# Moving VectorE's LayerNorm statistics of x1 from the front of a scan tile to its middle, with the power on GpSimd that follows them

## The chip, the cores and the metric

The kernel runs on one NeuronCore of a Trainium2 chip. The metric is the device time of one execution in microseconds (us). Below, PE is the matmul engine (TensorE), DVE is VectorE, ACT is ScalarE, POOL is GpSimd, and SP only issues DMAs. A trace of one execution shows when each instruction of each engine ran.

## What is computed

The block is a Mamba-2 mixer with an MLP, a LayerNorm, a gated ternary feed-forward network and a second LayerNorm, over 2 sequences of 2048 tokens with 256 features, in float32. Cut to what matters here:

```python
h   = x + mamba2(rmsnorm(x), ...)          # scan over chunks, 8 heads of 64
m   = square(relu(rmsnorm(h) @ w_fc)) @ w_proj
x1  = layernorm(x + (h + m))               # (v - mean) / sqrt(var + 1e-5)
f   = silu(x1 @ w1) * (x1 @ w2)
f   = gelu(gelu(f @ h1) @ h2) @ w3
out = layernorm(x1 + f)
```

## The kernel before

The 4096 tokens are 8 tiles of 512 tokens. A tile is 4 chunks of 128 tokens, one per pass of the partitions. Stage one, the scan, goes over the tiles in order (about the first half of the time) and writes x1 to DRAM. Stage two reads it back and does the feed-forward network; the change does not touch it.

In the scan each engine runs its own `iteration`, a list of calls written out by hand. Nothing reorders it: an engine does its instructions in the order in which they stand, and waits on semaphores for the others. The iteration of tile i mixes three tiles. It does the scan of tile i, the projection and convolution of tile i+1, and the MLP of tile i-1. The LayerNorm of x1 runs one tile further behind, for tile i-2. Tile 0 and tile 1 have no such LayerNorm, tiles 2 to 6 are one hardware loop, and tile 7 is written out by itself.

A chunk c of the scan passes through these steps (lines of the kernel before). PE makes the decay exponents (`exponents`, L665, called dlo and dhi), DVE clamps them into `E` (`mask_exponents`, L1448), ACT takes the exponential, and DVE multiplies with the scores (`scores`, L1458). PE's `y_diag` (L690) waits for that product and for `u`, which POOL makes (`make_u`, L1264). PE's `y_off` (L682) reads the state `S`. DVE adds the two (`y_off` L1466, `y_diag` L1477 and L1479) and gates the sum (`gate`, L1500). PE transposes it (`turn_y`, L703), ACT and DVE split it into a high and a low part (`yT`, DVE's L1351), PE multiplies by `w_out` (`out_rows`), and DVE adds the residual (`add_out`, L1511). After chunk 3, PE transposes `h` (`turn_h`, L720), DVE writes its low part (`hT`, also L1351), and PE's first MLP matmul (`fc(w, 0)`, L579 with `hT`) waits for it. POOL decays the state (`decay_state`, L1287) and makes `ud` (`make_ud`, L1271). DVE also runs 18 convolution taps per tile (`tap`, L1372) and normalizes the next x (`norm_x`, L1358). `ud` and the decay of chunk 3 are used by PE's `state(w, i, 3)` and DVE's `state`.

PSUM banks rotate. DVE's items share three banks, so PE may start an item only when DVE has drained the item three places before: dhi3 waits until `yT0` has been drained by L1351.

The part that is moved: `norm_x1` computes the LayerNorm statistics of x1, four BN_STATS (L177) and seven instructions on 128x4 values (L183 to L189), and signals `s_mv`. POOL's `x1_rstd` (L237) waits for `s_mv` and raises the variance to the power -0.5. DVE's `scale_x1` (L242), late in the tile, waits for POOL's result and writes x1, which SP stores.

Of the kernel before, what the change touches and what calls it, by code (L numbers as in the profile page):

```python
# [29 lines left out]
CH = TILE // P  # L30
# [15 lines left out]
EPS_LN = 1e-05  # L46
# [85 lines left out]
def post_ln_block(nc, x, x_t, w_in, conv_w, conv_b, dt_bias, a_log, d_skip, norm_w, w_out, w_fc, w_proj,  # L132
# [16 lines left out]
    with ctx:  # L149
        def sb(name, shape, dt=F32, into=ctx):  # L150
            return into.enter_context(nc.sbuf_tensor(name, shape, dt))

        def sem(name):
            return ctx.enter_context(nc.semaphore(name))
# [18 lines left out]
        def layer_norm_stats(step, src, bn, mv, eps):  # L173


            for c in range(CH):
                step.mark(nc.vector.bn_stats(bn[:, c, :], src[:, c, :]))  # L177
            step.wait(step.n)
            return layer_norm_tail(step, bn, mv, eps)

        def layer_norm_tail(step, bn, mv, eps):
            tt, ts = nc.vector.tensor_tensor, nc.vector.tensor_scalar
            step.mark(tt(mv[:, 0, :], bn[:, :, 1], bn[:, :, 4], ALU.add))  # L183
            step.mark(tt(mv[:, 2, :], bn[:, :, 1], bn[:, :, 4], ALU.subtract))
            step.link(tt(mv[:, 1, :], bn[:, :, 2], bn[:, :, 5], ALU.add))
            step.mark(ts(mv[:, 0, :], mv[:, 0, :], 0.5, None, ALU.mult))
            step.mark(tt(mv[:, 2, :], mv[:, 2, :], mv[:, 2, :], ALU.mult))
            step.link(ts(mv[:, 1, :], mv[:, 1, :], 1.0 / D, eps, ALU.mult, ALU.add))
            return nc.vector.scalar_tensor_tensor(out=mv[:, 1, :], in0=mv[:, 2, :], scalar=0.25,  # L189
                                                  in1=mv[:, 1, :], op0=ALU.mult, op1=ALU.add)  # L190

        STAT_STEPS = CH + 6
# [25 lines left out]
        def sum_x1(dve, t):  # L218

            dve.wait_ge(s_pj, KH * t + KH)  # L220
            dve.wait_ge(s_r2h, t + 1)
            dve.wait_ge(s_x1o, 16 * t + 1)
            dve.wait_ge(s_xh, t + 1)
            for c in range(CH):
                nc.vector.scalar_tensor_tensor(
                    out=x1[:, c, :], in0=pj_banks[c // 2][:, (c % 2) * D:(c % 2 + 1) * D],
                    scalar=r2h[:, c:c + 1], in1=xh[:, c, :], op0=ALU.mult, op1=ALU.add).then_inc(s_pjd, 1)

        def norm_x1(dve, t):
            step = Steps(dve, s_ls, STAT_STEPS * t)  # L230
            dve.wait_ge(s_pjd, CH * t + CH + 1)
            layer_norm_stats(step, x1, bn, mv, EPS_LN).then_inc(s_mv, 1)
            assert step.n == STAT_STEPS

        def x1_rstd(pool, t):
            pool.wait_ge(s_mv, t + 1)
            nc.gpsimd.tensor_tensor(rsv[:], mv[:, 1, :], eps[:, 3:4].broadcast_to([P, CH]), ALU.pow).then_inc(s_rsv, 1)  # L237
# [39 lines left out]
        bn, mv, rsv = sb("bn", [P, CH, 6]), sb("mv", [P, 3, CH]), sb("rsv", [P, CH])  # L277
        x1 = sb("x1", [P, CH, D])
# [32 lines left out]
        s_pjd = sem("proj_drained")  # L311
        s_xh = sem("x_plus_h_ready")
        s_r2h = sem("h_rstd_ready")
        s_mv = sem("ln_var_ready")
        s_rsv = sem("ln_rstd_ready")
        s_ls = sem("ln_step")
# [133 lines left out]
        with nc.Block() as block:  # L450
# [758 lines left out]
            def _(pool):  # L1209
# [36 lines left out]
                def m_lo_part(t, j):  # L1246
                    pool.wait_ge(s_mh, KH * t + j + 1)
                    nc.gpsimd.tensor_tensor(m_lo[:, j % MB, :], m_fc[:, j % 2, :], m_hi[:, j % MB, :].bitcast(F32),  # L1248
                                            ALU.subtract).then_inc(s_ml, 1)

                def chunk_totals(i):
                    pool.wait_ge(s_dec, i + 1)
                    nc.gpsimd.tensor_tensor(dec[:, 2, :], dec[:, 0, :], dec[:, 1, :], ALU.mult).then_inc(s_tot, 1)
# [7 lines left out]
                def make_u(w, i, c):  # L1261
                    turned_x(w, i, c)
                    ge(pool, s_si, CH * i + c - 1)
                    nc.gpsimd.tensor_tensor(heads(u[:, c % 2, :]), heads(xt[:, c % 2, :]),  # L1264
                                            bc(dt[:, c * HEADS:(c + 1) * HEADS]), ALU.mult).then_inc(s_u, 1)

                def make_ud(w, i, c):
                    pool.wait_ge(s_u, CH * i + c + 1)
                    if c == 0:
                        pool.wait_ge(s_dec, i + 1)  # L1270
                    nc.gpsimd.tensor_tensor(heads(ud[:, c % 2, :]), heads(u[:, c % 2, :]),  # L1271
                                            bc(dec[:, 1, c * HEADS:(c + 1) * HEADS]), ALU.mult).then_inc(s_ud, 1)

                def make_skip(w, i, c):
                    turned_x(w, i, c)
                    if c >= 2:
                        pool.wait_ge(s_rsy, CH * i + c - 1)
                        pool.wait_ge(s_di, w.dve(f"yT{c - 2}") + 1)
                    nc.gpsimd.tensor_tensor(heads(y[:, c % 2, :]), heads(xt[:, c % 2, :]), bc(dskip_b[:]),
                                            ALU.mult).then_inc(s_skip, 1)  # L1280

                def decay_state(i, c):
                    b, o = c % 2, 1 - c % 2
                    pool.wait_ge(s_sup, CH * i + c + 1)
                    if c == 0:
                        pool.wait_ge(s_tot, i + 1)
                    nc.gpsimd.tensor_tensor(heads(S[:, o, :]), heads(S[:, b, :]),  # L1287
                                            bc(dec[:, 2, c * HEADS:(c + 1) * HEADS]), ALU.mult).then_inc(s_sdec, 1)

                def iteration(w, i, mlp, more, norm):  # L1290
                    make_skip(w, i, 0)
                    make_u(w, i, 0)
                    chunk_totals(i)
                    if mlp:
                        m_lo_part(i - 1, 2)
                    make_ud(w, i, 0)
                    if mlp:
                        decay_state(i, 0)
                    else:
                        pool.wait_ge(s_tot, 1)  # L1300
                    make_u(w, i, 1)
                    make_skip(w, i, 1)
                    make_ud(w, i, 1)
                    decay_state(i, 1)
                    if norm:
                        x1_rstd(pool, i - 2)
                    make_u(w, i, 2)
                    make_u(w, i, 3)
                    make_ud(w, i, 2)
                    decay_state(i, 2)  # L1310
                    make_skip(w, i, 2)
                    if mlp:
                        m_lo_part(i - 1, 4)
                    make_skip(w, i, 3)
                    if mlp:
                        m_lo_part(i - 1, 6)
                    if more:
                        make_ud(w, i, 3)
                        decay_state(i, 3)
                    m_lo_part(i, 0)  # L1320
                    if more:
                        decay_operands(w, i + 1)
# [9 lines left out]
            def _(dve):  # L1332
# [15 lines left out]
                def lo_part(w, name, hi, lo):  # L1348

                    dve.wait_ge(s_hi, w.hi(name) + 1)  # L1350
                    nc.vector.tensor_tensor(lo, banks[w.dve_bank(name)][:], hi.bitcast(F32),  # L1351
                                            ALU.subtract).then_inc(s_dd, 1)
# [149 lines left out]
                def yT(w, c):  # L1502
                    lo_part(w, f"yT{c}", flat3(yT_hi), flat3(yT_lo))

                def add_out(w, i, c):
                    b = item(w, f"wo{c}")
                    dve.wait_ge(s_rsy, CH * i + c + 1)
                    if c == 0:
                        dve.wait_ge(s_xres, 16 * i + 16)
                        ge(dve, s_r2h, i)  # L1510
                    nc.vector.scalar_tensor_tensor(out=h[:, c, :], in0=b[:, 0:D], scalar=rsy[:, c:c + 1],  # L1511
                                                   in1=x_res[:, c, :], op0=ALU.mult, op1=ALU.add).then_inc(s_dd, 1)
# [15 lines left out]
                def iteration(w, i, before, more, norm):  # L1528
                    mlp = before is not None
                    per = F_STEPS + CM_STEPS  # L1530
                    step = Steps(dve, s_ds, HEAD_STEPS + per * i - (1 if mlp else 0))
                    if norm:
                        norm_x1(dve, i - 2)
                    mask_exponents(w, 0)
                    if mlp and not norm:
                        turn_squares(i)
# [50 lines left out]
                    if more:  # L1587
                        tap(step, w, i + 1, 4, 1)
                    add_out(w, i, 1)
                    yT(w, 2)  # L1590
                    y_diag(step, w, i, 3)
                    if more:
# [37 lines left out]
                    if mlp:  # L1630
                        sum_x1(dve, i - 1)
# [18 lines left out]
                step = Steps(dve, s_ds, 0)  # L1650
# [437 lines left out]
```

## Time and profile before

| | us |
|---|---|
| median of 3 runs (1225.24 to 1225.66) | 1225.28 |
| the profiled execution | 1226.21 |
| its span, first to last instruction | 1224.50 |
| PE busy in the span | 1195.6 (98%) |
| DVE busy | 783.8 (64%) |
| ACT busy | 639.2 (52%) |
| POOL busy | 237.7 (19%) |

The profiled execution has 1.71 us around its span. DVE's 64% is an average over two unlike stages: in the scan its busy tenths are 8 and 9, in the second stage 3 to 6. Ends of matmuls are modelled, so PE may show as busy while it waits a little; where a matmul starts is what to read.

### The profile page before, as it was taken

To read this page: it belongs to the slowest core of one execution; us is meant where nothing else is said; L and a number is where in the kernel's file an instruction comes from. 1 tells how busy PE (TensorE), PEld (TensorE's weight loads), DVE (VectorE), ACT (ScalarE), POOL (GpSimd) and SP (SyncE) were. 2 spreads that over 40 slices of the span, in tenths; PEclk is the share of its full clock that TensorE was granted. 3 is DMA by queue.
4 is the path that set the end of the run, shared out by engine and by line. 5 is a ranking of instruction groups with operands and counts; after the bars stand their busy time and mean duration, and the time that the engine had idled before them with its cause. 6 is when DMAs were issued, how large, how long until landed. Compare 5 with 4: busy or idle time off the path is not lost.

```text
span 1224.5 us, 19168 instructions
## 1 busy us (share of the span) xinstructions
PE 1195.6 (98%) x6412; PEld 1003.1 (82%) x6412; DVE 783.8 (64%) x1370; ACT 639.2 (52%) x1199; POOL 237.7 (19%) x210
## 2 busy tenths in 40 slices
PE   8899999999999999999999999999999999999996
PEld 7677888888887888788888888888888888888885
DVE  6798898989999898855535337345363363543633
ACT  6687888878788878666224124142141331422420
POOL 0517253443435261720000000000000000000000
PEclk9999999999999999999999999999999999999998
DMA  8214131333324141334500202002002020020000
GB/s 294 71 65 126 65 81 72 105 99 101 105 78 128 58 124 64 99 128 172 211 1 1 52 1 51 0 0 51 0 6 45 0 51 0 0 51 0 18 1 19
DMA packets 92169, 79.40 MB, mean 65 GB/s; under 512 B 63200, under 2 KB 81760, under 8 KB 90208
## 3 DMA queue, kind: packets, MB, share of 16 engines
q1 hardware_dynamic: 92128, 78.86, 20.8%
q8 instruction: 25, 0.41, 0.1%
q14 instruction: 16, 0.13, 0.0%
HBM read 66.77 MB, written 25.70 MB: 76 GB/s over the span
## 4 chain that ended last, share of the span: by engine, by line
issue 53%; POOL 0%; DVE 0%; POOLq 0%; DVEq 0%
POOL rsv_b L1937 0%; DVE o_sb L2014 0%; POOLq L1935 0%; DVEq L1768 0%; POOL rsv L237 0%; POOLq L450 0%
## 5 line engine op out<-in xcount | busy, mean ns | idle before, releaser
L1921 ACT ACTIVATE full<-bank,scale 128x512 f32<-128x512 f32 x128 | 88.3, 690 | 383.0 <-PE bank L1830 383.0
L1830 PE MATMUL bank<-hB_hi,h_sb 128*128 128x512 f32 x512 | 199.6, 390 | 0.0
L1830 PE MATMUL bank<-hB_lo,h_sb 128*128 128x512 f32 x512 | 199.6, 390 | 0.0
L1830 PE MATMUL bank<-hA_hi,h_sb 128*128 128x512 f32 x512 | 199.3, 389 | 0.0
L1830 PE MATMUL bank<-hA_lo,h_sb 128*128 128x512 f32 x512 | 199.3, 389 | 0.0
L1983 DVE CAST hA_hi<-full 128x512 fp32r<-128x512 f32 x64 | 27.3, 427 | 173.1 <-ACT full L1921 173.1
L1937 POOL TENSOR_TENSOR rsv_b<-mv_b,eps 128x4 f32<-128x4 f32 x8 | 10.7, 1340 | 618.2 <-DVE mv_b L189 618.2
L1830 PEld LDWEIGHTS bank<-hA_hi,h_sb 128*128 128x128 f32 x512 | 96.1, 188 | 20.1
L1830 PEld LDWEIGHTS bank<-hA_lo,h_sb 128*128 128x128 f32 x512 | 96.1, 188 | 20.1
L1830 PEld LDWEIGHTS bank<-hB_hi,h_sb 128*128 128x128 f32 x512 | 96.3, 188 | 19.2
L1830 PEld LDWEIGHTS bank<-hB_lo,h_sb 128*128 128x128 f32 x512 | 96.2, 188 | 19.0
L1372 DVE SCALAR_TENSOR_TENSOR xc<-xp,conv_w_sb,xc 128x512 f32<-128x512 f32 x144 | 104.4, 763 | 0.5
L1950 DVE TENSOR_TENSOR hA_lo<-full,hA_hi 128x512 fp32r<-128x512 f32 x128 | 88.0, 687 | 3.0
L1983 DVE CAST hB_hi<-full 128x512 fp32r<-128x512 f32 x64 | 27.1, 424 | 97.7 <-ACT full L1921 97.7
L1957 DVE SCALAR_TENSOR_TENSOR full<-bank,scale,gate 128x512 f32<-128x512 f32 x64 | 48.0, 751 | 63.1 <-PE bank L1830 62.9
L579 PE MATMUL bank<-w_pj_hi,m 128*128 128x256 f32 x256 | 81.7, 319 | 0.0
L1914 ACT ACTIVATE gate<-bank,scale 128x512 f32<-128x512 f32 x64 | 44.1, 689 | 60.5 <-PE bank L1830 60.5
L1248 POOL TENSOR_TENSOR m<-m_fc,m 128x512 fp32r<-128x512 f32 x29 | 43.7, 1506 | 162.2 <-ACT m L1044 162.2
L581 PE MATMUL bank<-w_pj_hi,m 128*128 128x256 f32 x256 | 72.4, 283 | 0.0
L580 PE MATMUL bank<-w_pj_lo,m 128*128 128x256 f32 x256 | 72.3, 282 | 0.0
L690 PEld LDWEIGHTS bank<-u,E 128*128 128x128 f32 x512 | 60.2, 192 | 10.8 <-issue 10.5
L1830 PE MATMUL bank<-w_sb,hA_hi 128*128 128x256 f32 x256 | 63.1, 283 | 0.0
(231 smaller groups left out, 2967.6 us busy)
## 6 DMA issues: line engine op xcount, KB each, us to landing
chk_xh<-w_ffn SPq DMA_DIRECT2D x16, 704.0 KB, 4.2
ffn_raw<-w_ffn SPq DMA_DIRECT2D x8, 1408.0 KB, 7.0
h_sb<-ffn_raw SPq DMA_DIRECT2D x2, 4096.0 KB, 19.0
xT<-x_t SPq DMA_DIRECT2D x8, 512.0 KB, 3.9
x_res<-x SPq DMA_DIRECT2D x8, 512.0 KB, 3.8
x_rows<-x SPq DMA_DIRECT2D x8, 512.0 KB, 3.5
x_in<-x_rows SPq DMA_DIRECT2D x8, 512.0 KB, 4.7
x_in<-x SPq DMA_DIRECT2D x7, 512.0 KB, 4.7
```

The source lines that it names most:

```text
L579: pe.matmul(o, lo, rhi, start=first, stop=False, skip_group_check=True)
L580: pe.matmul(o, hi, rlo, start=False, stop=False, skip_group_check=True)
L581: return pe.matmul(o, hi, rhi, start=False, stop=last, skip_group_check=True)
L690: last = pe.matmul(b[:, hs], E[:, c % 2, n, :], u[:, c % 2, hs], start=True, stop=True)
L1248: nc.gpsimd.tensor_tensor(m_lo[:, j % MB, :], m_fc[:, j % 2, :], m_hi[:, j % MB, :].bitcast(F32), ALU.subtract).then_inc(s_ml, 1)
L1372: ins = nc.vector.scalar_tensor_tensor(out=xc[:, m, :], in0=xp[:, m, n:n + TILE], scalar=conv_w_sb[:, m, n:n + 1], in1=xc[:, m, :], op0=AL ...
L1830: ins = pe.matmul(o, a_, b_, start=first and n == 0, stop=last and n == 1, skip_group_check=True)
L1914: nc.scalar.activation(gate[:, j % 2, :], b[:], ACT.Silu, scale=scale[:, 0, j:j + 1]).then_inc(s_gd, 1)
L1921: nc.scalar.activation(full[:, n % FULL, :], b[:], ACT.Gelu, scale=scale[:, 1 + n // KH, n % KH:n % KH + 1]).then_inc(s_gd, 1)
L1950: nc.vector.tensor_tensor(lo, full[:, n % FULL, :], hi.bitcast(F32), ALU.subtract).then_inc(s_split, 1)
L1957: nc.vector.scalar_tensor_tensor(out=full[:, j % FULL, :], in0=t_bank(KD + j)[:], scalar=scale[:, 1, j:j + 1], in1=gate[:, j % 2, :], op0= ...
L1983: nc.vector.tensor_copy(hi[:, n % KH, :], full[:, n % FULL, :]).then_inc(s_shi, 1)
```

## The change

DVE: `norm_x1` no longer stands at the front of the iteration (before the first mask of the exponents). The same eleven instructions, split into two functions, now stand after `add_out(w, i, 1)` and before `yT(w, 2)`. POOL: `x1_rstd` no longer stands between `decay_state(i, 1)` and `make_u(w, i, 2)`. It stands after `m_lo_part(i - 1, 6)`, before `make_ud(w, i, 3)` and `decay_state(i, 3)`. `scale_x1` and the store stay. The copy of `norm_x1` that runs after the last tile stays.

```diff
+        def stats_x1(dve, t):
+            step = Steps(dve, s_ls, STAT_STEPS * t)
+            dve.wait_ge(s_pjd, CH * t + CH + 1)
+            for c in range(CH):
+                step.mark(nc.vector.bn_stats(bn[:, c, :], x1[:, c, :]))
+            return step
+
+        def norm_x1_tail(step):
+            step.wait(step.n)
+            layer_norm_tail(step, bn, mv, EPS_LN).then_inc(s_mv, 1)
+            assert step.n == STAT_STEPS
...
                     decay_state(i, 1)
-                    if norm:
-                        x1_rstd(pool, i - 2)
                     make_u(w, i, 2)
...
                         m_lo_part(i - 1, 6)
+                    if norm:
+                        x1_rstd(pool, i - 2)
                     if more:
                         make_ud(w, i, 3)
                         decay_state(i, 3)
...
-                    if norm:
-                        norm_x1(dve, i - 2)
                     mask_exponents(w, 0)
...
                     add_out(w, i, 1)
+                    if norm:
+                        x1_step = stats_x1(dve, i - 2)
+                    if norm:
+                        norm_x1_tail(x1_step)
                     yT(w, 2)
```

The 13 new lines shift the numbers of all later lines by 13 (L1264 becomes L1277).

POOL in the loop over tiles 2 to 6, from the decay of chunk 1 on, before (`u` is `make_u` of chunks 2 and 3, `rsv` is the power):

```order
L1287 TENSOR_TENSOR S<-S,dec 128x512 [waits state_updated]
L237 TENSOR_TENSOR rsv<-mv,eps 128x4 [waits ln_var_ready]
L1257 REGISTER_ALU
L1264 TENSOR_TENSOR u<-xt,sm 128x512 [waits state_item_ready,turned_x_of_chunk_2_loaded]
L1264 TENSOR_TENSOR u<-xt,sm 128x512 [waits state_item_ready,turned_x_of_chunk_3_loaded]
```

The same place of POOL now:

```order
L1300 TENSOR_TENSOR S<-S,dec 128x512 [waits state_updated]
L1270 REGISTER_ALU
L1277 TENSOR_TENSOR u<-xt,sm 128x512 [waits state_item_ready,turned_x_of_chunk_2_loaded]
L1277 TENSOR_TENSOR u<-xt,sm 128x512 [waits state_item_ready,turned_x_of_chunk_3_loaded]
L1281 REGISTER_ALU
```

`u` of chunk 2 now follows the decay of the state directly; the power no longer stands between them.

POOL later in the same tile, now, from the MLP's low part of block 6 on (before, the power's row was not there):

```order
L1261 TENSOR_TENSOR m<-m_fc,m 128x512 [waits m_hi_ready]
L250 TENSOR_TENSOR rsv<-mv,eps 128x4 [waits ln_var_ready]
L1281 REGISTER_ALU
L1284 TENSOR_TENSOR ud<-u,dec 128x512 [waits u_ready]
L1300 TENSOR_TENSOR S<-S,dec 128x512 [waits state_updated]
```

`ud` and the decay of chunk 3 are now queued behind a wait for DVE's statistics.

DVE in the middle of the tile, now, from chunk 1's output on (before, the first row was followed at once by the row of `yT_lo`):

```order
L1524 SCALAR_TENSOR_TENSOR h<-bank,stat,x_res 128x256 [waits y_rstd_ready,dve_item_ready]
L232 ISA
L234 BN_STATS bn<-x 128x6 [waits proj_drained]
L234 BN_STATS bn<-x 128x6 x3
L168 ISA
L183 TENSOR_TENSOR mv<-bn 128x4 [waits ln_step]
```

After it come the other six small instructions of the statistics, and then chunk 2's `yT_lo`, `y_diag` and gate, in the order of before.

## Rows read from the trace of the kernel before

**Rows 1.** Busy time by stretch, tile 2 and tile 7: us, PE, PEld, DVE, ACT, POOL, clock.

```profile
161.43:228.05 66.62, 66.29 (x408) 55.93 (x407) 59.45 (x99) 54.31 (x112) 28.67 (x24) 1.00 0.33 96
...
494.70:545.00 50.30, 47.21 (x313) 39.97 (x312) 39.63 (x66) 31.81 (x67) 22.32 (x19) 1.00 0.31 96
```

**Rows 2.** PE's instructions in time, first half of tile 2: start, us, instruction [idle before].

```profile
170.21 1.97 PE L690 MATMUL bank<-u,E 128*128 128x64 f32 x16
...
179.78 1.97 PE L690 MATMUL bank<-u,E 128*128 128x64 f32 x16
...
182.32 0.50 PE L665 MATMUL bank<-to_l,from_s 128*128 128x512 f32 x1 [0.28 <-DVE yT_lo L1351]
```

**Rows 3.** DVE's instructions in time, first half of tile 2.

```profile
162.14 1.40 DVE L177 BATCH_NORM_STATS2 bn<-x 128x6 f32<-128x256 f32 x4
...
165.27 0.17 DVE L189 SCALAR_TENSOR_TENSOR mv<-mv 128x4 f32<-128x4 f32 x1
...
168.78 1.33 DVE L1458 TENSOR_TENSOR E<-E,GB 128x1024 f32<-128x1024 f32 x1
...
177.02 1.53 DVE L1500 TENSOR_TENSOR y<-tmp,z_s 128x512 f32<-128x512 f32 x1
178.47 1.21 DVE L1458 TENSOR_TENSOR E<-E,GB 128x1024 f32<-128x1024 f32 x1
...
180.20 1.46 DVE L1358 TENSOR_TENSOR xT<-xT,x_rstd 128x1024 f32<-128x1024 f32 x1
```

**Rows 4.** POOL's instructions in time, first half of tile 2.

```profile
167.98 1.04 POOL L1287 TENSOR_TENSOR S<-S,dec 128x512 f32<-128x512 f32 x1
...
176.57 1.42 POOL L1287 TENSOR_TENSOR S<-S,dec 128x512 f32<-128x512 f32 x1 [2.42 <-DVE S L1488]
177.96 1.48 POOL L237 TENSOR_TENSOR rsv<-mv,eps 128x4 f32<-128x4 f32 x1
```

**Rows 5.** All engines in time, the same place in tile 1, which has no power.

```profile
109.93 1.49 POOL L1264 TENSOR_TENSOR u<-xt,sm 128x512 f32<-128x512 f32 x1
...
110.44 2.06 DVE L1458 TENSOR_TENSOR E<-E,GB 128x1024 f32<-128x1024 f32 x1
...
113.91 1.23 DVE L1358 TENSOR_TENSOR xT<-xT,x_rstd 128x1024 f32<-128x1024 f32 x1 [0.81 <-DMA x_rstd<-x_rstd_row]
```

**Rows 6.** DVE's instructions in time, second half of tile 2.

```profile
202.12 0.48 DVE L1511 SCALAR_TENSOR_TENSOR h<-bank,stat,x_res 128x256 f32<-128x256 f32 x1 [0.79 <-PE bank L581]
204.58 0.69 DVE L1351 TENSOR_TENSOR yT_lo<-bank,yT_hi 128x512 fp32r<-128x512 f32 x1 [1.98 <-ACT yT_hi L907]
...
206.50 0.69 DVE L1479 TENSOR_TENSOR tmp<-tmp,y 128x512 f32<-128x512 f32 x1
...
208.38 2.07 DVE L1372 SCALAR_TENSOR_TENSOR xc<-xp,conv_w_sb,xc 128x512 f32<-128x512 f32 x3
...
211.02 0.69 DVE L1351 TENSOR_TENSOR yT_lo<-bank,yT_hi 128x512 fp32r<-128x512 f32 x1 [0.18 <-ACT yT_hi L907]
...
215.66 0.48 DVE L1511 SCALAR_TENSOR_TENSOR h<-bank,stat,x_res 128x256 f32<-128x256 f32 x1
...
218.03 1.28 DVE L1351 TENSOR_TENSOR hT<-bank,hT 128x512 fp32r<-128x512 f32 x2
```

**Rows 7.** The tile `mv`: durations in ns, min/median/max over the kernel.

```profile
L185 DVE TENSOR_TENSOR mv<-bn x8: 153/1011/1016, 163.9 to 589.4; 128x4 f32<-128x4 f32 x8
...
L237 POOL TENSOR_TENSOR rsv<-mv,eps x8: 1006/1452/1476, 178.0 to 590.2; 128x4 f32<-128x4 f32 x8
```

**Rows 8.** DVE's instructions in time, tile 0.

```profile
68.98 4.10 DVE L1372 SCALAR_TENSOR_TENSOR xc<-xp,conv_w_sb,xc 128x512 f32<-128x512 f32 x3
```

**Rows 9.** PE's instructions in time, end of tile 2.

```profile
209.75 0.60 PE L703 MATMUL bank<-ident,y 128*128 128x128 f32 x4
...
216.68 1.03 PE L720 MATMUL bank<-ident,h 128*128 128x128 f32 x8
...
219.62 0.39 PE L579 MATMUL bank<-hT,w_fc_lo 128*128 128x512 f32 x1
```

## The prediction

> **What bounds the kernel now.** I read the busy shares first: PE 98%, DVE 64%. Then the stretches by tile [rows 1]: in the scan DVE is busy 59.5 of 66.6 us per tile, so 64% understates it there. PE is busy 66.3 of 66.6 us. So PE sets the time, the waits it has left are small, and DVE follows with little slack. Moving DVE work can therefore save next to nothing, but it can cost as soon as one DVE result comes too late for PE. Third, I read PE, DVE and POOL side by side in time for tile 2; tiles 3 to 6 repeat it 66.6 to 66.7 us apart. Three places matter.
>
> At 182.32 PE waits 0.28 us for `yT_lo` of chunk 0 [rows 2]. This is the only wait that the first half of the tile shows as such. At 179.78 PE starts `y_diag` of chunk 1 [rows 2]; it needs the scores product that ends at 178.47 + 1.21 = 179.68 [rows 3], so that product has no more than 0.1 us in hand. At 219.62 PE starts the first MLP matmul [rows 9], which needs `hT_lo`, ended at 218.03 + 1.28 = 219.31 [rows 6]: 0.3 us in hand.
>
> **How POOL and DVE share.** The DVE products whose two inputs both lie in SBUF and POOL's products take turns. The gate runs from 177.02 for 1.53 us [rows 3], though the same form takes 0.69 (L1479 at 206.50 [rows 6]); it ends 0.56 us after POOL's `S` ends at 176.57 + 1.42 = 177.99 [rows 4]. POOL in turn wins the next turn if it is waiting when DVE's product ends: `S` was ready at 176.57 and got in before the gate. Instructions that read PSUM, such as `yT_lo`, keep their 0.68 us.
>
> **The front of the tile, removed.** Four BN_STATS and seven small instructions go from 162.14 to 165.27 + 0.17 = 165.44, 3.3 us of DVE [rows 3]. What was late behind them? The masks come earlier, so PE's `y_off` of chunk 0 can start some 0.14 us sooner. But `y_diag` of chunk 0 at 170.21 [rows 2] follows the scores product, which ends at 168.78 + 1.33 = 170.11 [rows 3]. That is 1.09 us after POOL's decay of `S` ends at 167.98 + 1.04 = 169.02 [rows 4], and the decay does not move: POOL's chain before it waits for ACT, not for the statistics. So the gain at `y_off` is taken back at `y_diag`. I take 0 per tile, with a bound of 0.3 if DVE gets ahead of POOL there (0.14 and another 0.15 that `y_diag` waits).
>
> **POOL's power, removed from 177.96.** Its 1.48 us hardly hold back DVE: the scores product beside it runs 1.21 us, its fastest form [rows 3, 4]. It works as a spacer. When it goes, `make_u` of chunk 2 is ready at 178.0, waits for the gate to end at 178.55, and takes the turn before the scores product of chunk 1. Tile 1 has no power and shows exactly this: `u` from 109.93 to 111.42, the scores product 2.06 us long, ending 1.08 after `u` [rows 5]. Price: 2.06 - 1.21 = 0.85 us. Behind the product on DVE stand `y_off` 1, `norm_x` and `yT_lo` 0. `norm_x` gets back 1.46 - 1.23 = 0.23, since `u` no longer runs beside it [rows 3, 5]. PE's `y_diag` 1 starts 0.85 late, at 180.63, and its exponents at 182.32 come with `yT_lo`, 0.85 - 0.23 = 0.62 later. From there all engines are shifted by 0.62 alike, since POOL's next `u` and DVE's next product wait for PE. Five loop tiles: 5 x 0.62 = 3.1 us. Bounds: 0 (the product wins the turn) and 0.85 each. I take 0.62, for tile 1 measured both halves.
>
> [...]
>
> **The middle, DVE.** `add_out` 1 ends at 202.60, and DVE then idles 1.98 us until 204.58 [rows 6]. The statistics cost 3.3 us at the front, of which L185 alone waits 1.011 - 0.153 = 0.86 for POOL [rows 7]; here POOL is done early, so 2.4 us. They end at about 204.95, `yT_lo` 2 runs 0.3 to 0.4 late, and DVE's wait for PE behind it (L1479 starts at 206.50 in both cases) absorbs that. By themselves the statistics are hidden.
>
> **The middle, POOL.** The power starts at 205.0 and takes 1.01 us when it waits for nothing [rows 7]. Queued behind it stand `ud` 3 and the decay of chunk 3. Before, both were done when L1479 started at its free 0.69 [rows 6]; now `ud` runs 206.05 to 207.1 (1.04, as `S` in rows 4). L1479 at 206.50 must wait for it: it ends at 207.1 + 0.56 = 207.65 instead of 207.19. The decay goes next, 207.65 to 208.55 (0.9 us, as `u` behind the gate in rows 5). The tap waits: 209.1. The gate of chunk 3 follows, 209.7. Before, it ended where the next taps begin, about 208.45 [rows 6]. So DVE is 1.25 us late. That taps do pay for this is seen in tile 0, where three of them beside `ud` and the decay take 4.10 us [rows 8] instead of 2.07 [rows 6].
>
> PE's `turn_y` 3 at 209.75 [rows 9] is just reached. DVE recovers some 0.27 before `yT_lo` 3, where it idled for ACT [rows 6], and stays 1.0 late from there, as nothing else in its queue waits. `add_out` 3 ends at 216.14 + 1.0 = 217.14 [rows 6]; PE's `turn_h` at 216.68 [rows 9] starts 0.5 late. `hT_lo` ends at 219.31 + 1.0 = 220.31, so the MLP matmul of 219.62 starts at 220.36, 0.74 late in all. Later DVE waits for PE again and its lateness is gone. Five tiles: 5 x 0.74 = 3.7 us. Bounds: 0 (POOL's two products find gaps) and 1.25 each. I take 0.74.
>
> **Tile 7.** It has no taps and no `ud` 3, and PE idles 3.1 of its 50.3 us [rows 1], so most of the 0.85 at its scores product is covered. I take 0.2 between 0 and 0.85.
>
> **Sum.** 3.1 + 3.7 + 0.2 = 7.0 us. The profiled execution takes 1226.21 us, 1.71 more than its span, and would take 1233.2. It lies 0.93 above the median of 1225.28, so the median becomes 1232.3 us.
>
> **Rivals.** *(a) Only the early turn is lost.* If `ud` and the decay fit between DVE's instructions, or DVE's slack at the end is larger than I read, the second half costs 0: 1225.3 + 3.3 = 1228.6. For it: I place the power to 0.1 us by adding durations. Against: two POOL products of 1 us must go through a stretch in which DVE is busy without a gap.
>
> *(b) Only the late turn is lost.* If the scores product gets its turn before `u` 2, the first half costs 0: 1225.3 + 3.7 = 1229.0. Against it: tile 1 [rows 5].
>
> *(c) Nothing is seen.* Both are covered, PE keeps its chain: 1225.3.
>
> *(d) Faster.* The place is the first half. If the scores products win both turns, PE gains 0.29 at `y_off` 0 and `y_diag` 0 and 0.23 at 182.32, since `norm_x` and so `yT_lo` come earlier: 0.52 x 5 = 2.6 us, 1222.7. It decides once the product is ready before POOL's decay at 167.98. For it: DVE is relieved by 3.3 us just there, and the 1.98 us gap takes the block. Against it: the product also needs `y_off` from PE, which PE starts no more than 0.14 us earlier.
>
> *(e) Worse.* Both lose at their bounds, because the waits of PE add up rather than overlap: 5 x (0.85 + 1.25) + 0.85 = 11.4 us, 1236.7.
>
> **Chances.** Forecast (both turns lost) 0.50, (a) 0.14, (b) 0.10, (c) 0.11, (d) 0.07, (e) 0.08. The range 1226.0 to 1237.0 holds all but (c), (d) and a little beyond (e). A measurement of this kernel tells about 0.2% from no change, 2.45 us. Slower by more: forecast, (a), (b), (e), 0.82. Within: (c), 0.11. Faster: 0.07.
>
> **What would show it.** In tiles 2 to 6 of the changed kernel: the scores product of chunk 1 takes about 2.06 us instead of 1.21, with `u` 2 right before it; PE's `y_diag` 1 starts that much later after `turn_y` 0; `y_diag` 0 stands as before relative to the tile's start. BN_STATS follow `add_out` 1, and the whole block takes about 2.4 us. The power takes about 1.0; DVE's L1479 waits for `ud` 3 and takes about 1.15; the gate of chunk 3 ends some 1.2 us later; PE waits for DVE before `turn_h` and before the first MLP matmul. The tile's period becomes 68.0 us (66.6 + 0.62 + 0.74). The forecast is wrong if that period stays at 66.6, if the scores product keeps 1.21, or if PE's granted clock leaves 1.00 [rows 1]. The second stage should take what it took.

## The result and the profile after

| us | before | after |
|---|---|---|
| median of 5 runs each | 1225.24 | 1232.68 (1229.93 to 1234.35) |
| ratio, 95% interval | | 1.006 [1.0046, 1.0074] |
| the profiled execution | 1226.21 | 1233.16 |
| its span | 1224.5 | 1231.4 |

The change costs 0.6%: 7.4 us by the medians, 6.9 us by the spans of the two profiled executions. The forecast was 1232.3, slower.

The same view as in [rows 1], now of the changed kernel: busy time by stretch, for tile 2 and tile 7. (The stretch of tile 7 in [rows 1] begins 0.10 us after that tile's first matmul, so its length isn't compared here.)

```profile
161.60:229.50 67.90, 66.82 (x407) 55.78 (x406) 60.17 (x99) 54.34 (x112) 29.90 (x24) 1.00 0.31 94
501.06:551.50 50.44, 47.41 (x312) 40.07 (x311) 39.95 (x66) 31.62 (x67) 23.01 (x19) 1.00 0.32 94
```

Tile 2 takes 67.90 instead of 66.62 us. PE's busy time rises by only 0.5, so the rest is waiting. The clock stays at 1.00. All five loop tiles do the same, 67.87 to 67.90 against 66.62 to 66.66 before: from the start of tile 2 to the start of tile 7 it is 339.46 instead of 333.17 us, 6.3 more. Tile 7 adds 0.23 at its first MLP matmul. That is 6.5 of the 6.9 us by which the span grew. Tile 2 itself starts 0.17 later, and the remaining 0.2 comes after that matmul of tile 7; the runs don't say why.

All engines in time, changed kernel, tile 2 (lines are 13 higher than before, and those of the matmul helpers too). In this view and the others of all engines below I print the rows of POOL and DVE, and the rows of PE that matter; what PE, its weight loads, ACT and SP do between them is left out, and "..." stands for left-out rows of POOL and DVE. First the place of POOL's removed power:

```profile
168.18 1.04 POOL L1300 TENSOR_TENSOR S<-S,dec 128x512 f32<-128x512 f32 x1
...
168.79 1.51 DVE L1471 TENSOR_TENSOR E<-E,GB 128x1024 f32<-128x1024 f32 x1
...
176.76 1.43 POOL L1300 TENSOR_TENSOR S<-S,dec 128x512 f32<-128x512 f32 x1 [2.42 <-DVE S L1501]
177.21 1.53 DVE L1513 TENSOR_TENSOR y<-tmp,z_s 128x512 f32<-128x512 f32 x1
...
178.16 1.49 POOL L1277 TENSOR_TENSOR u<-xt,sm 128x512 f32<-128x512 f32 x1
178.66 2.06 DVE L1471 TENSOR_TENSOR E<-E,GB 128x1024 f32<-128x1024 f32 x1
...
180.82 1.97 PE L703 MATMUL bank<-u,E 128*128 128x64 f32 x16 [0.70 <-issue]
181.25 1.21 DVE L1371 TENSOR_TENSOR xT<-xT,x_rstd 128x1024 f32<-128x1024 f32 x1
```

The gate at 177.21 is as long as before. Behind it, the scores product of chunk 1 takes 2.06 us, not the 1.21 of [rows 3]: POOL's `u`, which stood behind the power [rows 4], now starts at 178.16, ahead of it. These are tile 1's numbers [rows 5]. PE's `y_diag` 1 follows the product with 0.70 us of idle time. The view puts this on "issue", but it starts 0.10 us after the end of the product (178.66 + 2.06 = 180.72), which it needs; the spacer experiment below shows that the product was the cause. `norm_x` then runs 1.21 instead of 1.46. At the front, PE's `y_off` 0 starts 0.06 us earlier in the tile (5.34 instead of 5.40), but the scores product of chunk 0 takes 1.51 and ends at 170.30, still 1.08 behind POOL's decay (169.22), and `y_diag` 0 stands at 8.81 us in the tile (8.78 before).

Second, the middle and the end of the tile:

```profile
202.91 0.49 DVE L1524 SCALAR_TENSOR_TENSOR h<-bank,stat,x_res 128x256 f32<-128x256 f32 x1 [0.78 <-PE bank L594]
203.32 1.40 DVE L234 BATCH_NORM_STATS2 bn<-x 128x6 f32<-128x256 f32 x4
...
205.44 0.16 DVE L189 SCALAR_TENSOR_TENSOR mv<-mv 128x4 f32<-128x4 f32 x1
205.54 0.69 DVE L1364 TENSOR_TENSOR yT_lo<-bank,yT_hi 128x512 fp32r<-128x512 f32 x1
205.69 1.03 POOL L250 TENSOR_TENSOR rsv<-mv,eps 128x4 f32<-128x4 f32 x1 [0.83 <-DVE mv L189]
206.57 0.69 DVE L1490 TENSOR_TENSOR y<-y,bank 128x512 f32<-128x512 f32 x1 [0.33 <-PE bank L703]
206.69 1.04 POOL L1284 TENSOR_TENSOR ud<-u,dec 128x512 f32<-128x512 f32 x1
207.29 0.99 DVE L1492 TENSOR_TENSOR tmp<-tmp,y 128x512 f32<-128x512 f32 x1
207.69 1.49 POOL L1300 TENSOR_TENSOR S<-S,dec 128x512 f32<-128x512 f32 x1
208.20 1.53 DVE L1385 SCALAR_TENSOR_TENSOR xc<-xp,conv_w_sb,xc 128x512 f32<-128x512 f32 x1
209.66 0.68 DVE L1513 TENSOR_TENSOR y<-tmp,z_s 128x512 f32<-128x512 f32 x1
...
210.55 0.60 PE L716 MATMUL bank<-ident,y 128*128 128x128 f32 x4
...
217.80 1.09 PE L733 MATMUL bank<-ident,h 128*128 128x128 f32 x8
...
219.64 1.28 DVE L1364 TENSOR_TENSOR hT<-bank,hT 128x512 fp32r<-128x512 f32 x2
...
220.98 0.50 PE L592 MATMUL bank<-hT,w_fc_lo 128*128 128x512 f32 x1
```

The statistics fill DVE's idle time behind `add_out` 1, and DVE still waits 0.33 for PE after them, so what DVE does next is not late by their own length. The experiments test this. But POOL's `ud` starts 45.09 us into the tile; before it was 42.58. Only 0.63 of these 2.5 us is the early turn. So `ud` and the decay run into L1492 (0.99 instead of the 0.69 of [rows 6]) and the tap (1.53 instead of 0.74). The gate starts at 209.66.

To compare kernels, I read four starts, in us after the tile's first matmul, in tile 2:

| | `y_diag` 1 | `turn_y` 3 | `turn_h` | first MLP matmul | loop period |
|---|---|---|---|---|---|
| before | 18.35 | 48.32 | 55.25 | 58.19 | 66.63 |
| after | 19.22 | 48.95 | 56.20 | 59.38 | 67.89 |
| lateness | 0.87 | 0.63 | 0.95 | 1.19 | 1.26 |

The table holds the whole story: 0.63 us from the first half, and another 0.6 between `turn_y` 3 and the tile's end. The period is the better measure for what follows: within one execution it repeats to 0.07 us in every kernel here but one (told below), while the tile loop starts at another moment in each execution (159.4 to 162.7 us in the traces here), and the total carries that too.

### The profile page after: what moved, and what is told of

The parts are those of the page before. It is cut to its first block, busy times and chain, and to the rows that moved or that the text cites. A ratio compares the mean times of both kernels' runs of the same rounds, so it can differ in the third digit from the quotient of the medians.

```text
span 1231.4 us, 19168 instructions
## 1 busy us (share of the span) xinstructions
PE 1199.8 (97%) x6412; PEld 1003.7 (82%) x6412; DVE 788.4 (64%) x1370; ACT 639.4 (52%) x1199; POOL 244.4 (20%) x210
## 4 chain that ended last, share of the span: by engine, by line
issue 53%; POOL 0%; DVE 0%; POOLq 0%; DVEq 0%
POOL rsv_b L1952 0%; DVE o_sb L2029 0%; POOLq L1950 0%; DVEq L1783 0%; POOL rsv L250 0%; POOLq L463 0%
## 5 line engine op out<-in xcount | busy, mean ns | idle before, releaser
L1385 DVE SCALAR_TENSOR_TENSOR xc<-xp,conv_w_sb,xc 128x512 f32<-128x512 f32 x144 | 108.3, 790 | 0.5
L703 PE MATMUL bank<-u,E 128*128 128x64 f32 x512 | 61.8, 274 | 4.6 <-issue 4.0
```

What stands on the lines that cost most here:

```text
L703: last = pe.matmul(b[:, hs], E[:, c % 2, n, :], u[:, c % 2, hs], start=True, stop=True)
L1385: ins = nc.vector.scalar_tensor_tensor(out=xc[:, m, :], in0=xp[:, m, n:n + TILE], scalar=conv_w_sb[:, m, n:n + 1], in1=xc[:, m, :], op0=AL ...
```

## The experiments

The theory has two parts, one for each place where POOL's queue changed: the early turn (`u` before the scores product of chunk 1) and the late turn (`ud` and decay of chunk 3 behind the power). Its rival puts the cost on DVE's moved block. Each ratio below is against runs of the kernel before that were made together with that experiment; their median was 1226.71 us for the first four, and 1224.98 to 1225.26 for the others. So the ratios can be compared, and totals of different experiments only within these groups. In the recorded expectations, e2 is the spacer and e8 is "`u` 2 behind `norm_x`, in the kernel before".

**Front statistics, late power.** The changed kernel with DVE's block back at the front.

```diff
                     step = Steps(dve, s_ds, HEAD_STEPS + per * i - (1 if mlp else 0))
+                    if norm:
+                        norm_x1(dve, i - 2)
...
                     add_out(w, i, 1)
-                    if norm:
-                        x1_step = stats_x1(dve, i - 2)
-                    if norm:
-                        norm_x1_tail(x1_step)
```

> The changed kernel with DVE's statistics back at the front of the tile; only POOL's power stays late. Theory A (turns between POOL and DVE: without the power as a spacer u of chunk 2 goes before the scores product of chunk 1): the first half stays late, the product takes 2.06 us, y_diag of chunk 1 starts 19.2 us after the tile's first transpose instead of 18.35. In the second half the power no longer waits for DVE, ud and the decay come 1 us sooner, DVE is at most 0.5 us late and PE sees nothing. Tile period 67.25 us, 3.1 to 3.4 us above the kernel before. Rival B (the first half is late because the statistics left the front and shifted the masks): product 1.21, period 66.6, same time as before.

Measured: 1229.85 us, ratio 1.0021 [1.0011, 1.0030], period 67.24. The scores product still takes 2.06 us and `y_diag` 1 stands at 19.22, though DVE's code is that of before. So the early turn is POOL's alone, and it costs 67.24 - 66.63 = 0.61 us per tile. Of the late turn PE sees nothing, since the power no longer waits for DVE's block in the middle: L1492 still takes 1.11 us beside the decay, but the tap behind it keeps its 0.74, and from `turn_y` 3 (48.94) to the first MLP matmul (58.81) it is 9.87 us as before.

**A spacer.** The changed kernel, with a power of constants where the real one had been.

```diff
                     decay_state(i, 1)
+                    if norm:
+                        nc.gpsimd.tensor_tensor(spare[:], eps[:, 2:3].broadcast_to([P, CH]),
+                                                eps[:, 3:4].broadcast_to([P, CH]), ALU.pow)
                     make_u(w, i, 2)
```

(The tile `spare` is new and nobody reads it.)

> The changed kernel plus one more power on POOL (128x4, on constants, into a spare tile) between the decay of chunk 1 and u of chunk 2. It is work that nobody needs. Theory A: it works as a spacer, the product of chunk 1 goes back to 1.21 us and the first half to its old times; the second half stays late by 0.65. Tile period 67.3 us, about 3.3 us above before and 3.2 below the changed kernel. Rival B: an additional POOL instruction changes nothing or costs; period 67.9 or more.

Measured: 1229.72 us, ratio 1.0022 [1.0012, 1.0032], period 67.29. All engines in time, this kernel, tile 2:

```profile
178.73 1.47 POOL L1320 TENSOR_TENSOR spare<-eps 128x4 f32<-128x4 f32 x1
179.25 1.21 DVE L1475 TENSOR_TENSOR E<-E,GB 128x1024 f32<-128x1024 f32 x1
180.19 1.17 POOL L1278 TENSOR_TENSOR u<-xt,sm 128x512 f32<-128x512 f32 x1
...
180.98 1.46 DVE L1375 TENSOR_TENSOR xT<-xT,x_rstd 128x1024 f32<-128x1024 f32 x1
```

An instruction whose result nobody uses shortens each loop tile by 0.6 us. The 1.21 and 1.46 of [rows 3] are back, and so is `u`'s 1.17, in the kernel before:

```profile
179.41 1.17 POOL L1264 TENSOR_TENSOR u<-xt,sm 128x512 f32<-128x512 f32 x1
```

What is left is the late turn, 67.29 - 66.63 = 0.66 us. The two parts add to 1.27; the changed kernel shows 1.26.

**The power behind `ud` and the decay.** The changed kernel with POOL's last steps exchanged, and the same with the spacer too.

```diff
-                    if norm:
-                        x1_rstd(pool, i - 2)
                     if more:
                         make_ud(w, i, 3)
                         decay_state(i, 3)
+                    if norm:
+                        x1_rstd(pool, i - 2)
```

> The changed kernel with POOL's power moved behind ud and the decay of chunk 3. Theory A: those two run at their old places, the gate of chunk 3 and hT_lo are late by nothing that PE sees, although the statistics stay in the middle; the first half stays late by 0.63. Tile period 67.25 us, 3.2 us above before. Rival C (the 2.3 us of statistics that DVE now has in the middle make it late): the period stays at 67.9 us and the time at 6 to 7 us above before.

> Both: the needless power as a spacer and the real one behind ud and the decay of chunk 3; the statistics stay in the middle. Theory A: both losses go, tile period 66.6 us, the time of before within 0.5 us. If the statistics at either place were worth anything by themselves, it would differ from before: below 66.4 if their leaving the front gains, above 66.8 if their standing in the middle costs.

Measured: 1234.22 us, ratio 1.0057 [1.0041, 1.0074], period 68.01 for the first; 1229.49, ratio 1.0028 [1.0015, 1.0041], period 67.42 for the second. Neither period is what the theory said (67.25 and 66.6). With the two products free to run at their old moment, the tile is no shorter than with the two behind the power. All engines in time, the kernel with both edits, tile 2:

```profile
201.06 1.39 DVE L234 BATCH_NORM_STATS2 bn<-x 128x6 f32<-128x256 f32 x4
...
202.54 1.05 POOL L1285 TENSOR_TENSOR ud<-u,dec 128x512 f32<-128x512 f32 x1
202.58 1.03 DVE L184 TENSOR_TENSOR mv<-bn 128x4 f32<-128x4 f32 x1
...
203.55 1.05 POOL L1301 TENSOR_TENSOR S<-S,dec 128x512 f32<-128x512 f32 x1
203.72 0.90 DVE L186 TENSOR_SCALAR mv<-mv 128x4 f32<-128x4 f32 x1
...
204.80 0.16 DVE L189 SCALAR_TENSOR_TENSOR mv<-mv 128x4 f32<-128x4 f32 x1
204.90 0.69 DVE L1368 TENSOR_TENSOR yT_lo<-bank,yT_hi 128x512 fp32r<-128x512 f32 x1
205.04 1.01 POOL L250 TENSOR_TENSOR rsv<-mv,eps 128x4 f32<-128x4 f32 x1 [0.44 <-DVE mv L189]
```

The victims are now the statistics. A 128x4 instruction that takes 0.16 us alone takes 1.03 beside `ud`, and L186 takes 0.90 beside the decay. From the first BN_STATS to L189's end the block takes 3.9 us (201.06 to 204.96) instead of the 2.3 it takes in the changed kernel (203.32 to 205.60), and `turn_y` 3 is 0.3 late (48.64). The gate of chunk 3 starts 47.56 us into the tile, 1.22 later than before; with the spacer alone it was 1.09. So the theory was short of a piece: the wait for `s_mv` had two effects, of opposite sign. It pushed the two products onto the gate, but it also kept them off the statistics. In every order tried so far that puts these two products beside DVE's busy stretch, some DVE instruction pays: L1492 takes 0.99 us in the changed kernel and 1.11 with the statistics in front, instead of 0.69, and here L184 takes 1.03 and L186 0.90.

Not every DVE instruction pays. L186, a TENSOR_SCALAR with one input, takes 0.90 us beside the decay instead of 0.17. The four BN_STATS (L234), which also read one input, take 1.40 us beside POOL's `m` in the changed kernel, and 1.41 (L177 at 587.78 in the kernel before) after the last tile, where POOL is idle. Why these two differ, no run here shows.

**`u` 2 behind `norm_x`.** The kernel with the power last, with a wait for DVE's `norm_x` in front of the third `u` (its signal `s_xn` is one that DVE already gives).

```diff
                     decay_state(i, 1)
+                    if more:
+                        pool.wait_ge(s_xn, i + 2)
                     make_u(w, i, 2)
```

> The power behind ud and the decay of chunk 3 (as in the run before), and POOL's u of chunk 2 waits until DVE has normalized the next x, so that it runs beside yT_lo and y_diag of chunk 1, which read PSUM. Theory A: the scores product of chunk 1 takes 1.21 us and norm_x 1.22 instead of 1.46, PE's wait at the exponents of chunk 3 (0.28 us before) nearly goes, tile period 66.4 us, 1 to 1.4 us below the kernel before. Rival: u of chunk 2 or 3 comes too late for y_diag of chunk 2 or meets the next product, period 66.6 or more.

Measured: 1229.62 us, ratio 1.0032 [1.0020, 1.0045], period 67.18. Both miss the expected 66.4 and 1 to 1.4 us less than before, because that was reckoned from a period of 66.6 with the power last, and the last experiment measured 67.42. The step itself is as expected: 67.18 against those 67.42, 0.24 less, with `y_diag` 2 at 29.87 instead of the 30.11 of the kernel before.

**No statistics at all.** The kernel before, with the statistics of tiles 2 to 7 left out (POOL's power then works on constants, set once ahead of the tiles in a line not shown, so the result is not the LayerNorm's).

```diff
                     if norm:
-                        norm_x1(dve, i - 2)
+                        dve.sem_inc(s_ls, STAT_STEPS)
+                        dve.sem_inc(s_mv, 1)
```

> The kernel before with the statistics of x1 left out in tiles 2 to 7 (not moved; mean and variance are constants there), the power at its old place. DVE has 3.3 us less per tile at the front. Theory A: worth nothing, because y_diag of chunk 0 waits for a scores product that waits for POOL's decay; y_diag 0 starts 8.8 us after the tile's first transpose as before, period 66.6, same time within 0.3 us. Rival D (the relieved front gains): y_diag 0 at 8.5, period 66.3 or less, 1.5 us or more below before.

Measured: 1225.84 us, ratio 1.0008 [0.9999, 1.0017], period 66.64. All engines in time, this kernel, front of tile 2:

```profile
166.71 1.05 POOL L1287 TENSOR_TENSOR S<-S,dec 128x512 f32<-128x512 f32 x1
...
167.33 1.51 DVE L1458 TENSOR_TENSOR E<-E,GB 128x1024 f32<-128x1024 f32 x1
```

3.3 us of DVE work are gone from the front and the period does not move. The scores product starts earlier and waits longer for POOL's decay: 1.51 us instead of 1.33, and again it ends 1.08 us behind the decay (168.84 against 167.76); `y_diag` 0 stands at 8.80. Nothing was to be gained by relieving DVE here.

**`ud` and the decay earlier.** The changed kernel with the spacer, and the two products ahead of `m_lo_part(i - 1, 6)` instead of behind it and the power.

```diff
                     make_skip(w, i, 3)
+                    if more:
+                        make_ud(w, i, 3)
+                        decay_state(i, 3)
                     if mlp:
                         m_lo_part(i - 1, 6)
                     if norm:
                         x1_rstd(pool, i - 2)
-                    if more:
-                        make_ud(w, i, 3)
-                        decay_state(i, 3)
```

> The changed kernel with the spacer of e2, and with POOL's ud and decay of chunk 3 taken out from behind the power: they run before the MLP's low part of block 6, beside DVE's three taps ahead of add_out 1. Theory A (each POOL product costs DVE one turn wherever DVE's products read SBUF twice): the three taps take 4.1 us instead of 2.18, of which 0.8 fall into DVE's wait for PE; the statistics' small instructions, L1479 and the tap of the second half run free; the gate of chunk 3 ends 0.85 late instead of 1.1, hT_lo 0.55 late; tile period 66.95 us, against 67.29 with the spacer alone. Rival C (the statistics in the middle make DVE late by themselves): period 67.3 or more.

Measured: 1224.67 us, ratio 0.9998 [0.9989, 1.0008], period 66.64, better than the 66.95 I expected (with taps of 4.1 us and a gate 0.85 late). All engines in time, this kernel, tile 2:

```profile
197.10 3.76 DVE L1389 SCALAR_TENSOR_TENSOR xc<-xp,conv_w_sb,xc 128x512 f32<-128x512 f32 x3
197.36 1.49 POOL L1285 TENSOR_TENSOR ud<-u,dec 128x512 f32<-128x512 f32 x1
198.82 1.49 POOL L1301 TENSOR_TENSOR S<-S,dec 128x512 f32<-128x512 f32 x1
...
201.17 1.39 DVE L234 BATCH_NORM_STATS2 bn<-x 128x6 f32<-128x256 f32 x4
...
203.29 0.16 DVE L189 SCALAR_TENSOR_TENSOR mv<-mv 128x4 f32<-128x4 f32 x1
203.39 0.69 DVE L1368 TENSOR_TENSOR yT_lo<-bank,yT_hi 128x512 fp32r<-128x512 f32 x1
203.53 1.01 POOL L250 TENSOR_TENSOR rsv<-mv,eps 128x4 f32<-128x4 f32 x1 [1.54 <-DVE mv L189]
```

The two products now meet three taps, which take 3.76 us for it instead of 2.18. But these stand ahead of `add_out` 1, for which DVE had idled 0.79 us [rows 6], and the 1.98 us idle behind it take the rest together with the statistics. The gate of chunk 3 starts 0.29 late and `turn_y` 3 on time (48.34). So in this order the statistics in the middle are free, as is the power at the tile's end. The cost of the change in the loop lies in where POOL's neighbours went.

**`u` 2 behind `norm_x`, in the kernel before.** The wait alone, in the same place, in front of the third `u`; the statistics and the power stand where they stood before.

> The kernel before, statistics and power at the front, with one wait more: POOL's u of chunk 2 waits until DVE has normalized the next x, and runs beside yT_lo and y_diag. Theory A: the scores product stays at 1.21, norm_x takes 1.22 instead of 1.46, PE's 0.28 us wait at the exponents of chunk 3 nearly goes; the second half is as before. Tile period 66.40 us, 1.2 us below before in all. Rival: the late u moves the collision to another product and the period stays 66.6.

Measured: 1223.19 us, ratio 0.9985 [0.9975, 0.9995], period 66.39. Expected were 66.40 and 1.2 us less; the medians differ by 1.8, and the interval of the ratio holds both. All engines in time, this kernel, tile 2:

```profile
176.38 1.48 POOL L237 TENSOR_TENSOR rsv<-mv,eps 128x4 f32<-128x4 f32 x1
...
178.63 1.21 DVE L1360 TENSOR_TENSOR xT<-xT,x_rstd 128x1024 f32<-128x1024 f32 x1
...
180.06 1.04 POOL L1264 TENSOR_TENSOR u<-xt,sm 128x512 f32<-128x512 f32 x1 [2.21 <-DVE xT L1360]
```

`norm_x` takes 1.21 instead of the 1.46 of [rows 3], and PE no longer waits its 0.28 us for `yT_lo` 0 [rows 2]. This is the one version here that is measurably faster than the kernel before, by 0.15%.

**The decay of chunk 0 behind `u` 1 too.**

```diff
-                    if mlp:
-                        decay_state(i, 0)
-                    else:
+                    if not mlp:
                         pool.wait_ge(s_tot, 1)
                     make_u(w, i, 1)
+                    if mlp:
+                        decay_state(i, 0)
```

(The wait of the last experiment stays.)

> As e8, and POOL's decay of chunk 0 moves behind u of chunk 1, away from the scores product of chunk 0. Theory A: that product takes 1.21 instead of 1.33 and y_diag of chunk 0 starts at 8.65 instead of 8.8 us; y_diag of chunk 1 follows; tile period 66.25 us, 1.9 us below before. Rival: the chain u, decay, y, ud of POOL is 1 us longer where DVE has L1479 and m_lo, and DVE loses more there than PE gains: 66.6 or more.

Measured: 1224.63 us, ratio 0.9996 [0.9987, 1.0006]. The front does what was expected: `y_diag` 0 at 8.67 instead of 8.78. But the periods are 66.73, 66.73, 66.75, 66.14, 66.10, and not the expected 66.25: two kinds of tile in one execution of one program. First, all engines in time in tile 3, of the slow kind:

```profile
250.36 1.04 POOL L1264 TENSOR_TENSOR u<-xt,sm 128x512 f32<-128x512 f32 x1 [1.08 <-PE bank L697]
250.38 2.10 DVE L1365 TENSOR_TENSOR xnT_lo<-xT,xnT_hi 128x1024 fp32r<-128x1024 f32 x1
```

And in tile 5, of the fast kind:

```profile
383.85 2.14 POOL L1264 TENSOR_TENSOR u<-xt,sm 128x512 f32<-128x512 f32 x1 [1.23 <-PE bank L697]
383.87 1.22 DVE L1365 TENSOR_TENSOR xnT_lo<-xT,xnT_hi 128x1024 fp32r<-128x1024 f32 x1
```

POOL's `u` 3 and DVE's product start 0.02 us apart, POOL's first in both tiles. In one tile POOL gets the turn (1.04, and DVE 2.10), in the other DVE (1.22, and POOL 2.14), and the period is 0.6 us apart. Tiles 2 and 4 are like tile 3, tile 6 is like tile 5. What shifts the balance between tiles the runs don't show.

**Both places mended.** The changed kernel with `ud` and the decay ahead of `m_lo_part(i - 1, 6)`, as above, and the wait for `norm_x` in place of the spacer.

> The changed kernel with both collisions taken out and its own idea kept: the statistics stay in the middle, the power at the tile's end; ud3 and decay3 go back ahead of m_lo(6), and the third u waits for norm_x, so that Pool takes its turn at neither scores(1) nor norm_x. The theory (each collision is a price of its own, and the statistics themselves cost nothing in the middle) says both gains add: a loop period of 66.40 us, as with the wait alone in the kernel before (66.39), scores(1) at 1.21 us, the gate of chunk 3 at its old distance less 0.24 us, and about 1.3 us less than the kernel before in all. Against it: if the two mended places interact (the wait moves ud2, decay2 and what stands behind them on Pool later, onto the statistics or the taps), the period stays at 66.6 or goes above it, and the time is that of the kernel before or longer.

Measured: 1224.58 us, ratio 0.9995 [0.9986, 1.0004], period 66.40. The two gains add as the theory says, and the loop is as short as with the wait alone (66.39). The medians differ by 0.7 us, not by the expected 1.3, and the total is not told from the kernel before. Tile 7 keeps its 0.23 (it has no wait and no spacer).

## Why the prediction was right

**Right in mechanism and total.** 1232.68 against 1232.3, and a period of 67.89 against 68.0. Its two terms were shown apart: take the collision out of one place, and only the other's price stays (67.29 and 67.24). That the total is met to 0.4 us is partly luck: the five runs of the changed kernel lie 4.4 us apart, and the loop came out 0.5 us shorter than forecast while 0.4 us came outside it that no term stood for (0.17 before tile 2, 0.2 at the end).

**The front.** Predicted 0, found 0, and shown by taking the statistics away altogether. The reason given, that the product in front of `y_diag` 0 ends at a fixed distance behind POOL's decay whenever DVE is ready, holds: 1.09 us before, 1.08 in the changed kernel and without statistics. PE's `y_off` 0 gained 0.06 us, not 0.14.

**The early turn.** Predicted 0.62 from tile 1, found 0.61. Reading the same place in a tile that lacks the instruction gave both the 2.06 and the 1.23 us. That the power itself hardly holds the product back is confirmed as well: the product takes 1.21 us beside the real power [rows 3, 4] and 1.21 beside the spacer. The power is the one that waits: 1.48 us where the gate still runs, 1.03 at its new place.

**The late turn.** Predicted 0.74, found 0.66; this term was a little too large. The gate of chunk 3 starts 48.06 us into tile 2, against 46.34 before; less the early 0.63 that is 1.09 late, and 1.09 again with the spacer (47.43), not 1.25. The power started 0.1 us earlier than I placed it, and L1492 took 0.99, not 1.15. `turn_h` was 0.32 late instead of 0.5, and `hT_lo` ended 0.81 late (220.92, less the tile's start and the 0.63) instead of 1.0. So the first MLP matmul was 0.56 late, not 0.74. But the lateness did not end there: by the start of the next tile another 0.07 to 0.10 us is added, which the prediction put at nothing. It comes right behind the wait: that first MLP matmul takes 0.50 us instead of the 0.39 of [rows 9], and the next one starts 0.33 us behind it (221.31) instead of 0.23 (219.85).

**Tile 7.** Predicted 0.2, found 0.23. It is the early turn's: with the spacer, which tile 7 has too, its first MLP matmul stands at 48.59, against 48.85 in the changed kernel and 48.62 before. The 0.2 was chosen between two bounds and not worked out.

**Left out.** I asked what the moved wait does to the instructions behind it, and not what it spares the instructions beside it. Without the wait the statistics themselves would have met `ud` and the decay. The forecast did not need this, but "the power in front of the two products costs 0.74" was not the same as "putting it behind them gives 0.74 back": it gave back less than nothing, with 68.01 instead of 67.89.

**Against the rivals.** (a), the early turn alone, describes the run with the statistics in front and the late power (67.24), and (b), the late turn alone, the one with the spacer (67.29); neither describes the change. (c) is refuted by the result. (d) needed DVE to win both turns: the run without statistics shows nothing won at chunk 0, and in the changed kernel the product of chunk 1 loses its turn (2.06). (e) needed the bounds, and both terms stayed below them.

## What to carry to other kernels

In this kernel VectorE and GpSimd both work on operands in SBUF, and each move of a GpSimd product changed which DVE instruction paid for it, or whether one did: the scores product took 2.06 us instead of 1.21 behind `u` 2, and three taps 3.76 instead of 2.18 beside `ud` 3 and the decay. Where that may be so, list for each GpSimd product the DVE instruction that it meets before and after, and whether that one has slack. A short GpSimd instruction may be holding a long one back at a useful moment (here a 128x4 power of 1.48 us ahead of `u` 2, worth 0.6 us per tile); before it is moved, look what is next in its queue. And 3.3 us per tile less for DVE, at a place where PE waited for a product that waited for GpSimd, was worth nothing, while a changed order cost 1.26.

## What the runs showed that I had not expected

- The price of a collision did not grow with DVE's instruction: a 128x4 instruction of 0.16 us took 1.03 beside a 128x512 product of POOL, and the 128x1024 product 2.06 instead of 1.21, 0.87 and 0.85 more. It was less where POOL's product was further on: L1492 took 0.99 instead of 0.69.
- POOL's 128x4 power, 1.0 to 1.5 us long, did not hold back the DVE product beside it (1.21).
- A useless instruction made the loop 0.6 us per tile faster, by its place alone (68.01 to 67.42 with the power last).
- With the two starts 0.02 us apart, both outcomes occurred in one execution, 0.6 us per tile apart.
